# Mixture of experts around attention: tables made inside the selection, two blocks normalised by VectorE, and the shared unit at the head of its group

## The reference, cut to what matters

```python
x = x + 0.5 * ffn(layernorm(x)); x = x + attention(layernorm(x)); x = x + 0.5 * ffn(layernorm(x))

def ffn(x):                                   # 2048 tokens, width 128
    shared = (x1 * silu(x2)) @ shared_w2.T    # x1, x2 = split(x @ shared_w1.T); 2 x 384 wide
    gates = softmax(x @ wg.T)                 # 64 experts
    w_topk, idx_topk = top_k(gates, 8); w_topk = w_topk / sum(w_topk)
    # the pairs (token, choice) sorted by expert; each expert takes its first 160
    buf[expert, rank] = x[token]              # rank < 160
    out = expert_w2(x1 * silu(x2)) for each expert, x1, x2 = split(buf @ expert_w1.T)
    return shared + sum over choices of w * out
```

## Time and profile before

| what | us |
|---|---|
| median of 3 runs | 1018.36 (1017.56 to 1018.57) |
| profiled execution, device time | 1016.16 |
| its span, first to last instruction | 1014.4 |
| set-up block | 0 to 6.6 |
| selection f1 | 6.6 to 62.1 |
| wait for the first gathers, f1 | 62.1 to 71.5 |
| experts f1, to the last scatter | 71.5 to 291.0 |
| attention | 297.7 to 694.6 |
| selection f2 | 694.9 to 748.9 |
| experts f2, to the last scatter | 758.0 to 975.8 |
| weighted sum | 982.5 to 1014.4 |

### The profile page before, as it was taken

How to read it: one execution, slowest core, us unless ns; L and a number is a source line. 1 busy time by engine, 2 the same in 40 slices (tenths; PEclk the granted TensorE clock), 3 DMA queues, 4 the chain that set the end, 5 groups by cost and what they waited for, 6 DMA issues and landing times. The chain is left out here.

```text
span 1014.4 us, 20228 instructions
## 1 busy us (share of the span) xinstructions
PE 874.3 (86%) x6488; PEld 771.6 (76%) x6488; DVE 626.3 (62%) x1622; ACT 524.1 (52%) x1404; POOL 433.2 (43%) x436
## 2 busy tenths in 40 slices
PE   2649999999913999999999999996649999999917
PEld 2549999999913777777777777775639999999914
DVE  6936743333308989898989988784943643333317
ACT  4323333333301888888888888885323333333307
POOL 4035777777521222222222222221036777777520
PEclk9559999999966999999999999997559999999968
DMA  8807777777326200000000000005106777777327
GB/s 287 340 24 241 231 235 235 233 229 232 103 97 225 83 2 2 0 0 0 0 0 0 0 0 0 1 2 202 52 19 185 233 235 233 232 229 237 99 100 294
DMA packets 45478, 130.68 MB, mean 129 GB/s; under 512 B 8242, under 2 KB 17012, under 8 KB 45300
## 3 DMA queue, kind: packets, MB, share of 16 engines
q1 hardware_dynamic: 34320, 107.75, 32.0%
q0 software_dynamic: 10240, 20.99, 6.5%
q10 hardware_dynamic: 868, 1.31, 0.4%
HBM read 108.01 MB, written 22.02 MB: 128 GB/s over the span
## 5 line engine op out<-in xcount | busy, mean ns | idle before, releaser
L720 DVE TENSOR_TENSOR f_ehid<-f_esil,ps 128x480 f32<-128x480 f32 (+1 forms) x160 | 101.4, 634 | 261.2 <-ACT f_esil L605 248.4
L532 PE MATMUL ps<-f_xgT,f_ring 128*128 128x160 f32 x1536 | 234.0, 303 | 1.7 <-ACT f_xgT L592 1.7
L481 POOL DMA_INDIRECT f_xg<-xn_rows,f_take x160 | 164.1, 1026 | 147.8 <-issue 146.6
L532 PEld LDWEIGHTS ps<-f_xgT,f_ring 128*128 128x128 f32 x1536 | 217.6, 193 | 2.5 <-issue 2.5
L605 ACT ACTIVATE f_esil<-ps 128x480 f32<-128x480 f32 (+1 forms) x160 | 88.7, 554 | 237.1 <-PE ps L532 237.1
L492 POOL DMA_INDIRECT y_rows<-f_og,f_put x160 | 160.9, 1006 | 79.5 <-issue 45.7
L947 POOL TENSOR_TENSOR at_m<-at_m 128x512 f32<-128x512 f32 x64 | 82.1, 1283 | 260.6 <-DVE at_m L1110 260.6
L1300 ACT ACTIVATE at_prob<-ps,at_nmax 128x256 f32<-128x256 f32 x256 | 117.7, 472 | 48.7 <-DVE at_nmax L1117 48.6
L549 PE MATMUL ps<-f_ehid,f_ring 128*128 128x160 f32 x768 | 125.4, 299 | 1.2 <-DVE f_oT L733 1.2
L549 PEld LDWEIGHTS ps<-f_ehid,f_ring 128*128 128x128 f32 x768 | 110.5, 190 | 1.4 <-DVE f_ehid L720 1.4
L1129 DVE TENSOR_SCALAR at_prob<-at_prob,at_rinv 128x256 f32<-128x256 f32 x128 | 107.2, 877 | 2.3
(11 more groups left out here) (155 smaller groups left out, 1475.1 us busy)
## 6 DMA issues: line engine op xcount, KB each, us to landing
f_ring<-in_wexp SPq DMA_DIRECT2D x128, 576.0 KB, 5.0
y_rows<-zeros SPq DMA_DIRECT2D x16, 512.0 KB, 6.0
at_yt<-y_rows SPq DMA_DIRECT2D x8, 1024.0 KB, 4.9
ws_yt<-y_rows SPq DMA_DIRECT2D x8, 1024.0 KB, 12.4
f_xg<-xn_rows,f_take POOLq DMA_INDIRECT x160
y_rows<-f_og,f_put POOLq DMA_INDIRECT x160
xn_rows<-f_xn SPq DMA_DIRECT2D x8, 256.0 KB, 11.5
f_later<-in_wqkv SPq DMA_DIRECT2D x1, 1536.0 KB, 6.6
```

What stands on the lines that cost most here:

```text
L481: nc.gpsimd.indirect_dma_start(xg[:, G % SG, c, :], None, xn_dram, bass.IndirectOffsetOnAxis(take[:, n:n + 1], 0), bounds_check=last_token ...
L532: mm = nc.tensor.matmul(ps[:, HB + 2 * (u % 2) + half, f * w:(f + 1) * w], weights[:, half * FFN + f * P:half * FFN + (f + 1) * P], moving ...
L720: nc.vector.tensor_tensor(hid[:, u % 2, 0:w], sil[:, u % 2, 0:w], ps[:, HB + 2 * (u % 2), 0:w], ALU.mult).then_inc(ac, 1)
```

## The change

It has seven parts.

- Tables: `choice_no`, `iota_p` and `iota_c` leave the set-up block. GpSimd makes them in the selection of f1 (`clear_y` is true there alone), after its last product; `one_hot(0)` waits for them. `choice_no` becomes float, and the sum and the maximum at the end go over floats (`row_k`).
- VectorE normalises blocks 0 and 1 (a new `normalise` with subtract and multiply, which needs the power but not the product with the mean), between the moments. ScalarE keeps blocks 2 and 3. `normed` becomes two semaphores.
- ScalarE's `exps(0)` goes ahead of `normalise(3)`.
- The gate weights are stored once: 64 columns instead of 128.
- The shared unit is r = 0 of its group, the experts are r = 1 to 4. `up(0, 0)` stands ahead of `turn_in(0, 0)`; the copy `shared_in` is done for the next group. The asides on VectorE change units.
- `turn_out` part 0 waits for `GE` outputs of the group, which are now the shared one and three experts', part 1 for all five.
- In the last group `turn_out` and `group_out` part 0 follow the down-product of the last but one unit, part 1 that of the last.

```diff
 @block.gpsimd                                  # selection
+                    if clear_y:
+                        for table, pattern in ((iota_c, [[1, COLS], [0, TOPK]]), (iota_p, [[1, P], [0, TOPK]]),
+                                               (choice_no, [[1, TOPK], [0, COLS]])):
+                            nc.gpsimd.iota(table[:, :, :], pattern, base=0, channel_multiplier=0,
+                                           allow_small_or_imprecise_dtypes=True).then_inc(tables, 1)
 @block.vector
+                    def normalise(c):
+                        v.wait_ge(rstd, 2 * c + 1)
+                        for t in tiles(c):
+                            last = nc.vector.tensor_scalar(xn[:, t, :], x[:, t, :], mv[:, t, 0:1], st[:, 1, t:t + 1],
+                                                           ALU.subtract, ALU.mult)
+                        last.then_inc(normed_v, 1)
...
+                        if t == 0 and clear_y:
+                            v.wait_ge(tables, 3)
...
-                    for c in range(BLOCKS):
-                        moments(c)
+                    moments(0)
+                    moments(1)
+                    normalise(0)
+                    moments(2)
+                    normalise(1)
+                    moments(3)
                     less_max(0)
...
-                    then(nc.vector.tensor_tensor(by_k[:, :, :], by_k[:, :, :], choice_no[:, :, :], ALU.add))
-                    then(nc.vector.tensor_reduce(tg[:, 0, :], by_k[:, :, :].rearrange("p k c -> p c k"), AX.X, ALU.max))
+                    then(nc.vector.tensor_tensor(row_k[:, :, :], by_k[:, :, :], choice_no[:, :, :], ALU.add))
+                    then(nc.vector.tensor_reduce(tg[:, 0, :], row_k[:, :, :].rearrange("p k c -> p c k"), AX.X, ALU.max))
 @block.scalar
-                    normalise(0)
-                    normalise(1)
                     take_x(0)
                     normalise(2)
                     take_x(1)
+                    exps(0)
                     normalise(3)
-                    exps(0)
                     take_x(2)
 # experts
             def expert(u):
-                return u // GU * GE + u % GU if u % GU < GE else None
+                return u // GU * GE + u % GU - 1 if u % GU else None
 @block.tensor
-                        pe.wait_ge(os_, GU * G + GE)
+                        pe.wait_ge(os_, GU * G + GE + part)
...
+                            if last and u >= UNITS - 2:
+                                turn_out(i, g, u - UNITS + 2)
+
+                    up(0, 0)
                     turn_in(0, 0)
-                    up(0, 0)
 @block.scalar
-                            if r == 2:
-                                shared_in(i, g)
-                                if not (last and g == SG - 1):
-                                    group_in(*((i, g + 1) if g < SG - 1 else (i + 1, 0)))
+                            if r == 2 and not (last and g == SG - 1):
+                                shared_in(*((i, g + 1) if g < SG - 1 else (i + 1, 0)))
+                                group_in(*((i, g + 1) if g < SG - 1 else (i + 1, 0)))
...
+                    shared_in(0, 0)
+                    silu(0, 0)
                     group_in(0, 0)
-                    silu(0, 0)
 @block.vector
-                        elif i == 0 and u == GE:
+                        elif i == 0 and u == 0:
                             gate_sum()
                             gate_share()
-                        elif i == 0 and u == UNITS - 1:
+                        elif i == 0 and u == GU:
                             key_of()
 # build, set-up block
-                nc.gpsimd.iota(choice_no[:, :, :], [[1, TOPK], [0, COLS]], base=0, channel_multiplier=0)
...
-                nc.gpsimd.iota(iota_p[:, :, :], [[1, P], [0, TOPK]], base=0, channel_multiplier=0,
-                               allow_small_or_imprecise_dtypes=True)
-                nc.gpsimd.iota(iota_c[:, :, :], [[1, COLS], [0, TOPK]], base=0, channel_multiplier=0,
-                               allow_small_or_imprecise_dtypes=True)
```

More of the change, by code:

```diff
@@ L126, in experts @@
             by_k = rsb("by_k", [P, TOPK, COLS], I32)
+            row_k = rsb("row_k", [P, TOPK, COLS])
             tg = rsb("tg", [P, 3, COLS], I32)
-            wgsb = rsb("wgsb", [P, P])
+            wgsb = rsb("wgsb", [P, EXPERTS])
             pconst, wg_in = rsem("pconst"), rsem("wg_in")
-            var, rstd, normed, own = rsem("var"), rsem("rstd"), rsem("normed"), rsem("own")
+            var, rstd, own, tables = rsem("var"), rsem("rstd"), rsem("own"), rsem("tables")
+            normed_v, normed_a = rsem("normed_v"), rsem("normed_a")
             tps, tsa, logit = rsem("tps"), rsem("tsa"), rsem("logit")
@@ L144, in cols, with normed @@
                 return slice(c * TPBLK, (c + 1) * TPBLK)
+            def normed(c):
+                return (normed_v, c + 1) if c < 2 else (normed_a, c - 1)
             with nc.Block() as block:
@@ L154, in _ @@
                     for c in range(BLOCKS):
-                        sp.wait_ge(normed, c + 1)
+                        sp.wait_ge(*normed(c))
                         sp.dma_start(rows[:, cols(c), :], xn[:, cols(c), :]).then_inc(xn_stored, 16)
@@ L194, in logits @@
                     def logits(c):
-                        return ps[:, LOGB + c % 2, :].rearrange("p (t e) -> p t e", e=P)[:, :, 0:EXPERTS]
+                        return ps[:, LOGB + c % 2, 0:TPBLK * EXPERTS].rearrange("p (t e) -> p t e", e=EXPERTS)
                     def ranks(c):
@@ L308, in turn @@
                     def turn(c):
-                        pe.wait_ge(normed, c + 1)
+                        pe.wait_ge(*normed(c))
                         after(pe, tsa, c - 1)
@@ L320, in logits @@
                         for j, t in enumerate(tiles(c)):
-                            mm = nc.tensor.matmul(ps[:, LOGB + c % 2, j * P:(j + 1) * P], xnT[:, t * P:(t + 1) * P],
-                                                  wgsb[:, :], start=True, stop=True)
+                            mm = nc.tensor.matmul(ps[:, LOGB + c % 2, j * EXPERTS:(j + 1) * EXPERTS],
+                                                  xnT[:, t * P:(t + 1) * P], wgsb[:, :], start=True, stop=True)
                         mm.then_inc(logit, 1)
@@ L386, in normalise @@
                                                         scale=st[:, 1, t:t + 1])
-                        last.then_inc(normed, 1)
-                    normalise(0)
-                    normalise(1)
+                        last.then_inc(normed_a, 1)
                     take_x(0)
@@ L525, in up @@
                             pe.wait_ge(w_landed[e], 16 * i + 16)
-                            if r == 0:
+                            if r == 1:
                                 pe.wait_ge(xg_s, SG * i + g + 1)
-                            weights, moving, w = ring[:, e, :], xgT[:, g, r * CAPACITY:(r + 1) * CAPACITY], CAPACITY
+                            weights, moving, w = ring[:, e, :], xgT[:, g, (r - 1) * CAPACITY:r * CAPACITY], CAPACITY
                         after(pe, ac, U - 1)
@@ L582, in _ @@
                     step(STEPS - 1, False, True)
-                    turn_out(STEPS - 1, SG - 1, 0)
-                    turn_out(STEPS - 1, SG - 1, 1)
                 @block.scalar
@@ L590, in group_in @@
                         act.wait_ge(xg_t, G + 1)
-                        after(act, hb, GU * (G - 2) + GE)
+                        after(act, hb, GU * (G - 1))
                         nc.scalar.copy(xgT[:, g, :], ps[:, XB:XB + 2, :].rearrange("p b c -> p (b c)")[:, 0:GW]
@@ L596, in shared_in @@
                         G = SG * i + g
-                        after(act, hb, GU * (G - 1))
+                        after(act, hb, GU * (G - 2) + 1)
                         nc.scalar.copy(xs[:, g, :], xnT[:, bass.ds(G * P, P)]).then_inc(xs_in, 1)
@@ L629, in step @@
                                 group_out(*((i, g - 1) if g else (i - 1, SG - 1)), r)
+                            if last and u >= UNITS - 2:
+                                group_out(i, g, u - UNITS + 2)
+                    shared_in(0, 0)
+                    silu(0, 0)
                     group_in(0, 0)
-                    silu(0, 0)
                     step(0, True, False)
@@ L637, in _ @@
                     step(STEPS - 1, False, True)
-                    group_out(STEPS - 1, SG - 1, 0)
-                    group_out(STEPS - 1, SG - 1, 1)
                 @block.vector
@@ L725, in output @@
                         v.wait_ge(ob, U + 1)
-                        if r == GE:
+                        if r == 0:
                             xt = x[:, bass.ds(SG * i + g, 1), :].rearrange("p a d -> p (a d)")
@@ L730, in output @@
                         else:
-                            if r == 0:
+                            if r == 1:
                                 after(v, og_t, 2 * (SG * i + g - 1))
```

(6 more changed lines are left out.)

## The result

| what | us |
|---|---|
| changed kernel, median of 4 runs | 1007.39 (1005.85 to 1008.40) |
| kernel before, the 4 runs beside them | 1018.27 (1017.56 to 1018.57) |
| ratio | 0.9888, 95% interval 0.9874 to 0.9903 |
| profiled execution after: time, span | 1007.05, 1005.3 |

What follows compares the result with a forecast made beforehand. TensorE was taken as full inside the expert stages, so only their edges could pay: 4.0 + 2.5 + 0.6 + 2.6 + 1.3 + 0.6 = 11.6 us, from 1018.36 to 1006.8, range 1002 to 1011.

Steps and rivals of the forecast that it cites:

- Start of selection, 2.4: First stage, first moments to choosing: choosing at +9.8 instead of +12.2 us, 2.4 us gained.
- The mask, −1.3: First selection: VectorE's mask tensor_scalar waits until GpSimd's iota_p ends at 16.4, costing 1.3 us (bounds 0 to −2.0).
- rival (a): First selection: the tables hold nothing and the mask runs at once; gain 12.9 us, 1005.5; chance 0.20.
- rival (b): First selection: tables hold VectorE throughout, MAX8 and replacements too; 2.2 us more lost, 1010.3 with late x; chance 0.10.
- Second selection, 2.6: Second expert stage's selection: choosing at about 703.2 instead of 705.81, 2.6 us gained (2.2 to 3.1).
- Shared unit in the hole, 1.3 a stage: Stage start: shared up-product runs while TensorE awaits the first gathered group, taking 1.3 us off its queue per stage.
- last turns, 0.6 a stage: Stage end: part 0 turned before the last down-product, first scatter sooner; 0.6 us per stage (0.3 to 0.8).
- Rival (d): Stage starts: early shared unit leaves TensorE at 1.2 GHz longer, 1.3 us goes back per stage, 1009.4; chance 0.06.
- The collision, −0.5: First stage start: the moved f_later load runs beside group 0's last gathers, delaying the fifth by 0.5 us (0 to 2).
- rival (c): First stage start: moved load collides, fifth gather 2 us late, 1.5 us more lost, 1008.3; chance 0.08.
- Attention unchanged: Attention stage between the two expert stages: untouched and assumed only to shift, 0 us gained or lost.
- Rival (e): Expert loops: TensorE stands still in each of 32 groups; at 0.5 us a group 4.4 slower, 1022.8; chance 0.04.

Runs made afterwards that it cites:

- b_tables: Changed kernel with choice_no made in set-up, iota_p before the first power, only iota_c behind the last product; 1006.02 us, ratio 0.9868.
- b_later: Changed kernel with the f_later load released when group 0 is gathered and transposed, instead of by the shared up-product; 1005.26 us, ratio 0.9863.
- c_before: The kernel before, run again unchanged for a second profiled execution; 1018.13 us against 1018.35, ratio 0.9995.
- both: Changed kernel with f_later loaded behind the first gathers and the tables moved where nobody works beside them, on another chip; 1204.15 us, ratio 0.9894.

## Why the prediction was right, and by how much each step was off

The total holds: 11.6 forecast, 10.9 measured (9.9 to 12.8 by the interval), inside the range and with the sign. It holds because the steps were nearly all the right ones. That it holds so closely is in part luck: in the profiled executions the gain is 9.1, short of the forecast by 2.5, of which 1.8 lies around the start of attention, where the forecast had nothing. One of the signs of being wrong came true as well: the first five gathers needed 9.48 us, over the 8.1 that were named.

- **Set-up, 2.9:** 2.86. The first quarter of x lands 2.9 us after its issue and is what comes last.
- **Start of selection, 2.4:** 2.51. Four normalisations by VectorE take 1.10, as read from attention. The logits' part of the sum was wrong: I counted 0.3 for half the columns and it is 0.1. The chain was not bound by it, since VectorE with its moments and normalisations comes last.
- **The mask, −1.3:** −1.07 by itself (`b_tables`), −0.90 in the piece. That the iota holds this `tensor_scalar` to its end was right, and rival (a), tables that hold nothing, fell by the 1.36 us row; so did rival (b), by MAX8 and replacements that keep their times. I let the mask run its 0.29 behind the iota; in fact it ended 0.14 after it, which is the difference. Two rows without an `iota` beside settle the cause: 0.29 for the mask (`b_tables`) and 0.11 for `value` (1.85 before). The bounds of the first selection (2.6 to 5.4) are not what its terms give: a late x and a hold by all three tables would leave 2.0 of the 5.3, no hold 5.3. Nothing else hung on them.
- **Second selection, 2.6:** 3.20 in this profile, 2.74 in the four kernels where choosing came at 8.13. The mechanism was right. The 0.46 between the two is the clock: here it stays at 1.00 for some 3.3 us into the stage and the first four transposes take 0.66, in `b_later` it falls after 1.5 us and they take 1.12. It comes with a later rise behind the gathers: where choosing comes at 7.67, the first expert's up-product to the next transposes takes 7.7 to 7.8 us, where it comes at 8.13, with the same order of units, 6.5 to 6.7.
- **Shared unit in the hole, 1.3 a stage; last turns, 0.6 a stage:** together 1.9 forecast. In f1 the piece up-product to last scatter gained 3.32, of which 1.46 is the wait for `f_later` (the same fourteen groups took 181.84 before, 180.38 after); 1.86 is left. In f2 it gained 1.23. The difference is the clock: in f2 it stayed at 0.50 some 1.8 us longer than before. Rival (d) is thus true for about a third of its 1.3, in one of the two stages; over all profiles but those of the last group the first expert's up-product to the next transposes ranges from 6.4 to 7.8 us with the new order (fourteen stages, mean 7.1) and 8.3 to 9.4 with the old (six stages, mean 8.7). The mean gain is 1.6 a stage, so this term was a little low and not too high. At the end alone the gain is 0.31, not 0.6: the turns give 0.93, but I had the last unit's extra work at 0.4 and it is 0.62.
- **The wait for `f_later`, 1.7:** 1.46.
- **The collision, −0.5:** −1.39. This is the mis-sized term. The step that failed is "most of the bytes move before its issue": the load keeps the DMA engines at 0.78 to 1.01 from 62 to 67, and the fifth gather goes at 64.43. By then at most 0.6 MB had moved (82, 340 and 430 GB/s in the three rows above, gathers included), of the load's 1.5 MB. From that issue to the transposes it takes 4.0 us, and 2.6 in `b_later` (64.39 to 66.98), where the load is elsewhere. The upper bound of 2 us was sound, and rival (c) with its 1.5 more is nearly what happened (0.9 more); I had given it 0.08. The repair is `b_later`, with transposes after 8.05 us.
- **Attention unchanged:** not quite. VectorE waited 7.0 us instead of 6.3 for its first load of expert outputs; from the stage's start to its first power it is 14.0 to 14.4 us in every kernel with the new selection and 13.4 to 13.6 in those without. Why is open. Batch 0 took 28.06 instead of 26.90, and here most of the difference is the clock of the execution. Its length goes with the recorded clock, whatever the kernel: 26.9 where the clock is 1.00 from 13 us behind the first power on, 27.7 to 28.1 where it falls again from about 20 to 23 (`c_before` is one of these four), 28.8 where it rises only at 18.7, 29.7 to 29.9 where it rises late and falls again. The late rise is seen in nine of the twelve profiles with some part of the change and in neither of the two without; whether the time of arrival brings it isn't settled.
- **Rival (e), a wait in the loop:** fell. Group period 12.88 us in both kernels, TensorE without a gap.

The median's gain (10.9) is larger than the profiled one (9.1), since the profiled execution before was 2.1 below its median and the one after 0.3 below its own.

## What to carry to other kernels

A transfer that is moved into a quiet time of the compute engines is moved into a busy time of the queues if that quiet is itself a wait for transfers: look at who else has bytes on the way there, and release the load by the landing of those (here one changed wait, 1.4 us back). A table made by GpSimd costs next to nothing where VectorE runs moments, MAX8 or replacements, and up to its full length where a short `tensor_scalar` stands: place it by the neighbour's instruction, not by GpSimd's free time. And an edit of two microseconds is to be judged by its piece of the timeline where whole runs spread by more than that, with the clock of the compared pieces beside it.

## What the runs showed of the hardware that was not expected

- Beside an `iota` of 1.93 us a `tensor_scalar` of 0.29 is recorded as 1.36, to 0.14 after its end, and one of 0.11 as 1.85; beside GpSimd's power of 1.05 us VectorE's four normalisations (also `tensor_scalar`) take 1.10, no more than two in 0.60 would give, and MAX8 keeps its 0.61 beside an iota. The Trainium skill (Advanced Engine Details and Errata, VectorE Performance Modes) says that GpSimd and VectorE's two-port instructions block each other at a shared port; the mask row agrees with it, and `b_tables` (0.29 where no iota runs) too. The normalisations don't show it; which forms are two-port ones no run here tells.
- Eight f32 matrix products with 64 columns take 1.97 us, with 128 columns 2.08. This is at the lower clock (the transposes beside them take 1.12 and 1.11, not 0.66); at the higher one no row compares them.
- In f1 the page's clock reads 1.00 where twelve up-products take 3.54 us, exactly as at a recorded 0.50 in `both`. Durations show the clock where its record doesn't.
- The same program moved some 145 GB/s in its expert stages on one chip and 235 on another, and took 1200.7 us instead of 1007.4, with its DMA engines less busy and not more. No row here shows the cause. The Trainium skill (HBM Reference, Specifications (TRN2)) says that two cores share a memory domain and that, when both stream, each gets about 358 GB/s; that is more than this kernel's 235, so by this figure of the Trainium skill a neighbour alone would not explain the 145 (an estimate). Whether one was at work no run here shows.
